# A second gather stage in which VectorE and ScalarE copy twelve tiles of rows per twenty slots instead of ten, and ScalarE reads its places two to a word

## The reference

```python
msg = relu(x[src] + edge_attr)
agg = segment_sum(msg, dst, num_segments=x.shape[0])
h = (1.0 + eps) * x + agg
x = layernorm(x + relu(h @ W.T + b))
```

## Time and profile before

| | us |
|---|---|
| three runs | 7807.85, 7809.77, 7810.02 |
| the profiled execution, its own time | 7809.06 |
| its span, first to last instruction | 7807.2 |
| POOL busy in the span | 5374.0 (69%) |
| ACT busy | 5031.8 (64%) |
| DVE busy | 4478.2 (57%) |
| PE busy | 5327.4 (68%) |

### The profile page before, as it was taken

One profiled execution on the slowest core, in us unless ns is written; L12 is line 12 of the kernel. 1 busy time (PEld: TensorE's weight loads), 2 busy tenths in 40 slices (PEclk: granted clock), 3 DMA queues, 4 the chain that ended last, 5 costly groups with the idle time before them and its releaser, 6 DMA issues. The chain is left out here.

```text
span 7807.2 us, 195329 instructions
## 1 busy us (share of the span) xinstructions
PE 5327.4 (68%) x24390; PEld 3211.3 (41%) x24390; DVE 4478.2 (57%) x44173; ACT 5031.8 (64%) x41329; POOL 5374.0 (69%) x5600
## 2 busy tenths in 40 slices
PE   5666666665666666667995777776776777777676
PEld 3333333333333333336993444444443444444445
DVE  4666666666666666667995444444444444444445
ACT  4666666666666666665775666666666666666663
POOL 7777777777777777771004777777777777777774
PEclk6666666767766676668996555555555555555555
DMA  4333333333333333335772222222222222222221
GB/s 110 88 88 86 88 86 86 87 86 85 88 86 88 86 88 85 86 85 142 198 198 62 58 57 57 58 57 57 57 58 57 57 58 57 57 57 58 57 58 42
DMA packets 790838, 624.03 MB, mean 80 GB/s; under 512 B 537246, under 2 KB 618024, under 8 KB 788770
## 3 DMA queue, kind: packets, MB, share of 16 engines
q1 hardware_dynamic: 564136, 323.19, 16.1%
q0 software_dynamic: 178816, 186.37, 12.3%
q10 hardware_dynamic: 46450, 102.55, 3.8%
HBM read 502.00 MB, written 109.60 MB: 78 GB/s over the span
## 5 line engine op out<-in xcount | busy, mean ns | idle before, releaser
L578 POOL DMA_INDIRECT Z<-in_x_dram,src_idx x2791 | 2670.3, 957 | 863.5 <-issue 847.2
L1470 POOL DMA_INDIRECT X<-x_scratch,src_idx x2785 | 2656.4, 954 | 860.3 <-issue 829.1
L262 ACT ACTIVATE rows_by_act<-table 64x4 uint8 x19840 | 1955.5, 189 | 901.6 <-issue 901.6
L262 ACT ACTIVATE a_rows_by_act<-table 64x4 uint8 x19456 | 1917.8, 189 | 958.4 <-issue 958.4
L265 DVE TENSOR_REDUCE rows_by_dve<-table 64x4 uint8 x19840 | 1318.4, 139 | 1193.2 <-issue 1189.9
L265 DVE TENSOR_REDUCE a_rows_by_dve<-table 64x4 uint8 x19456 | 1292.8, 139 | 844.8 <-issue 842.6
L633 PE MATMUL PS<-ident,Z 128*128 128x128 f32 x2791 | 626.2, 372 | 1304.1 <-DMA Z<-in_x_dram,src_idx 1301.2
L1500 PE MATMUL PS<-X,ident 128*128 128x320 f32 (+1 forms) x1250 | 781.8, 726 | 992.0 <-DMA X<-x_scratch,src_idx 991.3
L662 PE MATMUL PS<-ZT,W_sb 128*64 128x320 f32 x2500 | 1287.5, 661 | 22.7 <-ACT ZT L715 22.5
L633 PEld LDWEIGHTS PS<-ident,Z 128*128 128x128 f32 x2791 | 422.9, 186 | 1515.6 <-issue 898.4
L1500 PEld LDWEIGHTS PS<-X,ident 128*128 128x128 f32 x1250 | 296.1, 294 | 1411.7 <-DMA X<-x_scratch,src_idx 1395.1
(11 more groups left out here) (163 smaller groups left out, 4535.2 us busy)
## 6 DMA issues: line engine op xcount, KB each, us to landing
Z<-in_edge_attr_dram SPq DMA_DIRECT2D x625, 160.0 KB
E<-in_edge_attr_dram SPq DMA_DIRECT2D x625, 160.0 KB, 2.2
h_scratch<-h_ring ACTq DMA_DIRECT2D x312, 320.0 KB
hT<-h_scratch SPq DMA_DIRECT2D x312, 320.0 KB
rows_sent<-in_x_dram SPq DMA_DIRECT2D x3840, 0.2 KB
rows_sent<-x_scratch SPq DMA_DIRECT2D x3840, 0.2 KB
Z<-in_x_dram,src_idx POOLq DMA_INDIRECT x2791
X<-x_scratch,src_idx POOLq DMA_INDIRECT x2785
```

The costliest lines, as they stand in the source:

```text
L262: return nc.scalar.activation(to, of, ACT.Copy)
L578: nc.gpsimd.indirect_dma_start(out=Z[:, r, j, 0:D], out_offset=None, in_=x, in_offset=bass.IndirectOffsetOnAxis(ap=src_idx[:, n:n + 1], ax ...
L1470: nc.gpsimd.indirect_dma_start(out=X[:, r, j, :], out_offset=None, in_=x1_dram, in_offset=bass.IndirectOffsetOnAxis(ap=src_idx[:, n:n + 1] ...
```

## The change

In the second gather stage VectorE and ScalarE copy six tiles each per pass, for the slots 8, 12, 16, 18, 20 and 24 of the first pass and those 20, 40, ... later (`C_DESTS`). The 24 steps of a pass are spread over its 20 slots by `steps_of`: slots 0, 5, 10 and 15 carry two. POOL gathers 87 tiles per pass.

ScalarE's places hold two to a word, 16 bits each and without `TABLE_AT`, in both gather stages: a step loads 16 words, and in front of each copy the half is taken out of the word (`& 65535` or `>> 16`) and the table's place is added. VectorE's words stay as they were. The second stage's places are loaded with twelve DMAs, one per tile.

```diff
-        C_EVERY = {BY_DVE: 4, BY_ACT: 4}
-        C_SLOT = {BY_DVE: 8, BY_ACT: 8}
-        C_TILES = {j: BODY // each for j, each in C_EVERY.items()}
+        C_DESTS = {BY_DVE: [8, 12, 16, 18, 20, 24], BY_ACT: [8, 12, 16, 18, 20, 24]}
+        C_TILES = {j: len(slots) for j, slots in C_DESTS.items()}
...
+        WORDS = {BY_DVE: P, BY_ACT: P // 2}
...
+        def load_copied_at_c(sp, loaded):
+
+            for j in (BY_DVE, BY_ACT):
+                for T, first in enumerate(C_DESTS[j]):
+                    sp.dma_start(copied_at[C_ROW[j] + T:C_ROW[j] + T + 1, :, 0:WORDS[j]],
+                                 copied_at_dram[j][first:first + BODY * (BODIES - 1) + 1:BODY, :].unsqueeze(0)
+                                 ).then_inc(loaded, 16)
...
         def copy_rows(engine, kind, first_row, k, T, step, copy, to, place, copied):
 
             row = first_row + T
+            packed = kind == mybir.EngineType.Activation
+            words = STEP // 2 if packed else STEP
+            low, high = (0, 2 ** 31 - 1) if packed else (TABLE_AT, TABLE_AT + WORD * (NODES - 1))
             _, columns = nc.values_load_multi_w_load_instructions(
-                copied_at[row:row + 1, ds(at(k, 1, 0), 1), step * STEP:(step + 1) * STEP].rearrange("o a n -> o (a n)"),
-                [kind], min_val=TABLE_AT, max_val=TABLE_AT + WORD * (NODES - 1),
+                copied_at[row:row + 1, ds(at(k, 1, 0), 1), step * words:(step + 1) * words].rearrange("o a n -> o (a n)"),
+                [kind], min_val=low, max_val=high,
                 skip_runtime_bounds_check_because="src holds numbers of nodes")
+            if packed:
+                columns = [(word >> 16 if half else word & 65535).with_bounds(min_val=0, max_val=WORD * (NODES - 1))
+                           for word in columns for half in (0, 1)]
             for n, column in enumerate(columns):
                 last = copy(to[:, place, step * STEP + n:step * STEP + n + 1].bitcast(mybir.dt.uint8),
-                            table_bytes[:, ds(column - TABLE_AT, WORD)])
+                            table_bytes[:, ds(column if packed else column - TABLE_AT, WORD)])
...
+                        halfwords = at_rows[:, 1, 0:S * WORDS[BY_ACT]].bitcast(mybir.dt.uint16)
+                        nc.vector.tensor_scalar(halfwords.rearrange("sb (q p) -> sb q p", q=S),
+                                                index_tiles(src_rows)[:, :, BY_ACT, :],
+                                                float(WORD), 0.0, ALU.mult, ALU.add).then_inc(at_made, 1)
...
+            def steps_of(s, j):
+
+                steps = C_TILES[j] * (P // STEP)
+                return [(n // (P // STEP), n % (P // STEP)) for n in range(steps) if n * BODY // steps == s]
...
-                            T, step = s // C_EVERY[BY_ACT], s % C_EVERY[BY_ACT]
-                            if slots == BODY and step < P // STEP:
-                                copy_rows(act, mybir.EngineType.Activation, C_ROW[BY_ACT], k, T, step, by_act, rows_act, T,
-                                          act_copied)
+                            if slots == BODY:
+                                for T, step in steps_of(s, BY_ACT):
+                                    copy_rows(act, mybir.EngineType.Activation, C_ROW[BY_ACT], k, T, step, by_act, rows_act, T,
+                                              act_copied)
```

More of the change, by code:

```diff
@@ L209, in gnn_kernel @@
         shares_out = ctx.enter_context(nc.semaphore("shares_out"))
-        copied_at_dram = {j: nc.dram_tensor(f"copied_at_scratch{j}", (G, P), int32, kind="Internal").ap()
+        WORDS = {BY_DVE: P, BY_ACT: P // 2}
+        copied_at_dram = {j: nc.dram_tensor(f"copied_at_scratch{j}", (G, WORDS[j]), int32, kind="Internal").ap()
                           for j in (BY_DVE, BY_ACT)}
         sent_at_dram = nc.dram_tensor("sent_at_scratch", (SB, P), int32, kind="Internal").ap()
+        def load_copied_at_c(sp, loaded):
[4 more added lines that the diff above has]
+                                 ).then_inc(loaded, 16)
         def load_copied_at(sp, j, row, first, each, loaded):
             tiles = BODY // each
-            sp.dma_start(copied_at[row:row + tiles, :, :],
+            sp.dma_start(copied_at[row:row + tiles, :, 0:WORDS[j]],
                          copied_at_dram[j][first:first + each * (tiles * BODIES - 1) + 1:each, :]
@@ L359, in _ @@
                         for n, j in enumerate((BY_DVE, BY_ACT)):
-                            halves_of_rows(sp, copied_at_dram[j].rearrange("(sb q) p -> sb (q p)", q=S), at_rows[:, n, :],
+                            halves_of_rows(sp, copied_at_dram[j].rearrange("(sb q) p -> sb (q p)", q=S), at_rows[:, n, 0:S * WORDS[j]],
                                            copied_at_stored)
@@ L409, in _ @@
                         dve.wait_ge(src_float, S)
[L410 to L413, removed]
+                        nc.vector.tensor_scalar(at_rows[:, 0, :].rearrange("sb (q p) -> sb q p", q=S),
+                                                index_tiles(src_rows)[:, :, BY_DVE, :],
+                                                float(WORD), float(TABLE_AT), ALU.mult, ALU.add).then_inc(at_made, 1)
+                        halfwords = at_rows[:, 1, 0:S * WORDS[BY_ACT]].bitcast(mybir.dt.uint16)
+                        nc.vector.tensor_scalar(halfwords.rearrange("sb (q p) -> sb q p", q=S),
+                                                index_tiles(src_rows)[:, :, BY_ACT, :],
+                                                float(WORD), 0.0, ALU.mult, ALU.add).then_inc(at_made, 1)
                         nc.vector.tensor_copy(sent_rows[:, :], index_tiles(src_rows)[:, SENT_SLOT % S, BY_SP, :]
@@ L1233, in _ @@
                 def _(sp):
-                    for j in (BY_DVE, BY_ACT):
-                        load_copied_at(sp, j, C_ROW[j], C_SLOT[j], C_EVERY[j], copied_at_in_c)
+                    load_copied_at_c(sp, copied_at_in_c)
                     for i in range(PIECES):
@@ L1405, in copied_in @@
             def copied_in(g, j):
-                return g >= C_SLOT[j] and (g - C_SLOT[j]) % C_EVERY[j] == 0
+                return g >= C_DESTS[j][0] and g % BODY in [slot % BODY for slot in C_DESTS[j]]
             def gathers_in(g):
@@ L1416, in copied_of, with copied_tile @@
                 return [j for j in (BY_ACT, BY_DVE) if copied_in(s if isinstance(k, int) and k == 0 else s + BODY, j)]
+            def copied_tile(s, j):
+                slots = C_DESTS[j]
+                if s in slots:
+                    return 0, slots.index(s)
+                return -1, slots.index(s + BODY)
+            def steps_of(s, j):
+                steps = C_TILES[j] * (P // STEP)
+                return [(n // (P // STEP), n % (P // STEP)) for n in range(steps) if n * BODY // steps == s]
             def copied_count(k, s, j):
-                return at(k, C_TILES[j], (s - C_SLOT[j]) // C_EVERY[j] + 1)
+                body, T = copied_tile(s, j)
+                return at(k, C_TILES[j], C_TILES[j] * body + T + 1)
             def copied_place(s, j):
-                return (s - C_SLOT[j]) // C_EVERY[j] % C_TILES[j]
+                return copied_tile(s, j)[1]
             def landed(g):
@@ L1550, in _ @@
                     act.wait_ge(x1T_even, CHUNKS)
-                    act.wait_ge(copied_at_in_c, 32)
+                    act.wait_ge(copied_at_in_c, 16 * sum(C_TILES.values()))
                     all_bodies(act, body)
@@ L1576, in body @@
                             add(k, s, firsts[s % S])
-                            T, step = s // C_EVERY[BY_DVE], s % C_EVERY[BY_DVE]
-                            if slots == BODY and step < P // STEP:
-                                copy_rows(dve, mybir.EngineType.DVE, C_ROW[BY_DVE], k, T, step, by_dve, rows_dve, T, dve_copied)
+                            if slots == BODY:
+                                for T, step in steps_of(s, BY_DVE):
+                                    copy_rows(dve, mybir.EngineType.DVE, C_ROW[BY_DVE], k, T, step, by_dve, rows_dve, T,
+                                              dve_copied)
                     for c in range(CHUNKS):
@@ L1586, in _ @@
                         one_hot(0, s)
-                    dve.wait_ge(copied_at_in_c, 32)
+                    dve.wait_ge(copied_at_in_c, 16 * sum(C_TILES.values()))
                     dve.wait_ge(x1T_even, CHUNKS)
```

## The result

The changed kernel takes 9481.22 us (median of 4 runs, 9480.91 to 9482.43); the kernel before took 7809.59 us in the runs beside it. The ratio is 1.2139, interval [1.2125, 1.2153]: 21% slower, where 7760 was forecast and 7850 was the upper end of the range. The profiled execution's span is 9480.6 us, against 7807.2.

A forecast was written before the change was run, and what follows sets the result against it. POOL's gathers were taken to bound the kernel; afterwards ScalarE's 109.8 us plus 0.6 for waits gave 110.4 us a pass, 1.6 less than 112.0, x 31 = 50 us off 7809.06: 7760 us, range 7729 to 7850.

The forecast's parts named there:

- the form and price of the arithmetic before a copy: ScalarE, before each copy: two register operations joined into one instruction of 37 ns, giving 98 ns per copy.
- the sum: ScalarE's second-stage pass: 24 steps 104.2 us, Relu work 2.8, loop's end 2.7; 109.8 us against POOL's 109.5.
- ScalarE's queue as the bound: Rival: arithmetic before the copies costs more than shorter loads and saved gathers give; 7884 us at 104 ns; chance 0.21.
- its point of decision, 100.9 ns: Per-copy pace at which ScalarE's second-stage pass reaches 112.0 us with no wait between the chains.
- its dearest case: In the ScalarE-queue rival, three operations in the instruction (46 ns): 107 ns per copy, a pass of 116.7 us, 7955 us.
- The first gather stage doesn't suffer: its steps finish sooner: First gather stage: ScalarE's new step was claimed no slower for the engine than the old; no time change given.
- whole-word step: ScalarE's unpacked step, priced at 0.075 + 1.972 + 0.056 + 3.06 = 5.16 us when the engine waits out the load.
- Packing takes 0.8 us off a step: ScalarE's step: packed 4.34 us against 5.16 us unpacked, as the engine sees it.
- POOL's part: Second gather stage: 62 gathers fewer at 1.2585 us each, 78 us in all, the most the change can give.
- VectorE hidden: Second gather stage: VectorE's pass of 101 us stays under POOL's 109.5, with 8 us to spare.
- SP's loads of the places: SP's queue: twelve DMAs in place of two, 0.31 us each, 3 us more ahead of the x1 stores; costs nothing.
- Instruction fetch: Rival: ScalarE's longer loop body stops at each further 256 instructions, about 8040 us; chance 0.04 together with VectorE as bound.

The follow-up runs named there:

- the last experiment: Changed kernel with ScalarE's 16 words a step each used for two copies, one joined multiplication and addition before each copy, half the rows wrong: 7793.17 us, ratio 0.9973.
- The single additions: Kernel before, with ScalarE's words lacking only the table's place, so one single addition stands before each copy; loads of 32 words: 8138.54 us, ratio 1.0422.
- the whole-word kernel: Changed kernel with only the packing undone: six tiles, ScalarE's places one to a word with the table's place in them: 7758.99 us, ratio 0.9934.
- half a load: Six plain tiles, but ScalarE loads 16 words a step and copies with each twice, no arithmetic between copies, half the rows wrong: 7759.94 us, ratio 0.9937.
- the six-tile kernel: Changed kernel with only the packing undone, so six tiles each and whole words for ScalarE: 7758.99 us, ratio 0.9934.
- the two experiments with one joined operation: One joined multiplication and addition before each copy: on the kernel before, 8192.4 us; on the changed kernel with 16 words each used twice, 7793.17 us.
- the single additions with half the load: Changed kernel with 16 words a step, each used for two copies, and one single addition before each copy, half the rows wrong: 7755.98 us, ratio 0.9927.

## Why the prediction was wrong

**The step that failed** is the form and price of the arithmetic before a copy: "Two adjacent ones appear as one instruction of 37 ns on ScalarE". The row showed that two operations can be joined, not that these two are. The mask stays apart from the addition, and the shift is joined with it into an instruction of 58 ns, so a copy costs 139.6 ns instead of 98. In the second stage this is 768 x 41.6 ns = 32.0 us a pass. With it, the sum closes: 109.8 + 32.0 - 24 x 0.076 (the load came out shorter) + 4.5 (breaks) = 144.5, against 145.1 measured. The rival that I had named, ScalarE's queue as the bound, is what happened, and its point of decision, 100.9 ns, was the right order: the 98 ns of the last experiment ended 0.3% faster, 128 ns was 15% slower. It was somewhat too high, as at 98 ns the pass is already level with the kernel before. Yet its dearest case was 107 ns, and my range ended at 102.5: both followed from the same row. I had even written that a half-word shift may take longer, and put no row beside it, since none has one.

**"The first gather stage doesn't suffer: its steps finish sooner"** was wrong, and is 676 us of the loss (620 up to its last gather). Twenty steps of 32 copies at 139.6 instead of 95.6 ns are 28.2 us more, less 20 x 0.945 us for the shorter load: 9.3. The measured pass is 22.1 longer. The single additions showed what is missing, a term for which the prediction had no place, as it charged the whole-word step with a load that nothing hides (5.16 us): 10.6 us a pass when the load loses its cover. 9.3 + 10.6 = 19.9. That test had whole-word loads, so the term is only near its size here; the last 2.2 us were not taken apart.

**"Packing takes 0.8 us off a step"** was wrong because of that cover. In the whole-word kernel the load lies mostly behind the copies; half a load is worth nothing there (7759.94 against 7758.99). So the packing had nothing to gain at all, whatever its price: six tiles fit without it.

**POOL's part** held in its mechanism: 62 gathers fewer, and a kernel that POOL bounds gains. Its size was 51 us, not 78, as a gather takes 10 ns more in the six-tile kernel (964 ns in the mean, 954 before). The number of tiles can't be the whole reason: with packed words and five tiles the mean is 963. Long gathers are more frequent in these kernels (194 over 1 us in the six-tile kernel, 112 before), and by the records nearly all of them overlap the TENSOR_TENSOR that makes VectorE's one-hot matrix, which overlaps a quarter of all gathers; that this is the cause was not tested.

**VectorE hidden** was right: its add into the table waits 950 us for PE. **SP's loads of the places** took longer than the 0.31 us of the earlier trace rows and were hidden all the same, as ScalarE's first load starts at 4907.2 us:

```profile
L218 SPq DMA_DIRECT2D copied_at<-copied_at_scratch x12: 538/721/11057, 4788.1 to 4810.6; - x12
```

**Instruction fetch** was priced at 3.5 stops of 2.6 us, 9.1 us a pass; the breaks that came cost 4.5. The unbroken runs of the earlier trace rows were no evidence against it: there the queue is ahead of the engine, and short stops wouldn't show. If the breaks are stops of the instruction stream, the rival was right in kind and is, in the second stage, some 140 us of the loss of 1672.

## What to carry to other kernels

Before packing data that an engine's queue reads as addresses, ask which work hides the load now: shortening a load that runs behind other work is worth nothing, and each instruction between two copies can take away that cover as well. A price read from one pair of operations belongs to that pair; where each copy multiplies it 768 times in a pass, the operations in question are to be found in a row, or bounded from instructions that stay apart. And where two edits come together, price each alone: here the sixth tile was worth 51 us and the packing cost 954 on its own.

## What the runs showed of the hardware

- Which register operations are joined into one instruction on ScalarE: multiplication and addition, 37 ns in the two experiments with one joined operation; right shift and addition, 58 ns in the changed kernel and 67 where the remainder replaces the mask; remainder and addition, 67 ns there. A mask and an addition stay two of 38 ns.
- Straight loop code is broken by stops of some 0.25 to 0.3 us. Counted in one pass of each gather stage of the changed kernel and of the last experiment, they stand 128 of ScalarE's instructions apart (256 where the one between doesn't fall between copies). For the single additions with half the load that is 59 copies with 59 additions, two loads, Relus and their arithmetic; in the changed kernel 49 copies with 74 register instructions. In the kernel before they don't show between copies, where the queue is ahead of the engine.
- The Trainium skill (Runtime: NRT & Kernel Launch, section Instruction fetch mechanics) says that the sequencer streams straight code by itself, with the cost of a block's end mostly hidden, and that a taken branch out of the blocks held stalls. The stop of 2.6 us at the loop's branch agrees with the second half. By the 16 breaks, 4.5 us of a pass of 145.1, the first half doesn't hold in full for ScalarE's loop here, if they are stops of the instruction stream, which their even count suggests and no run here proves.
- A copy of 64x4 bytes lasts 189 ns in the median in the kernel before, 191 where the queue sends one each 98 ns, and 205 in the changed kernel, where it sends one each 139.6. So in these runs the copies' duration alone shows whether the queue keeps up.
